# Keeping normalised tokens in SBUF, sending each expert result to its token's home row, and reading the results back with plain transfers

## What is computed

```python
x  = x + attention(...)                      # x2 in the kernel, B*N = 4096 tokens
xf = layernorm(x)                            # l2 in the kernel
shared = gelu(xf @ Wfc_s + bfc_s) @ Wproj_s + bproj_s
probs  = softmax(xf @ Wr)                    # 8 experts
topk_p, topk_i = top_k(probs, 2);  topk_p = topk_p / sum(topk_p)
for e in range(8):
    h = gelu(xf @ Wfc[e] + bfc[e]) @ Wproj[e] + bproj[e]
    routed = routed + h * gate[:, e:e+1]     # gate: topk_p of the two chosen experts, else 0
out = x + shared + routed
```

## Time and profile before

| | us |
|---|---|
| runs, median (lowest to highest of 3) | 2877.65 (2874.66 to 2878.85) |
| the profiled execution | 2873.23 |
| its span in the trace | 2871.6 |
| PE busy | 2529.7 (88% of the span) |
| DVE busy | 1781.9 |
| ACT busy | 1677.4 |
| POOL busy | 1298.8 |

### The profile page before, as it was taken

One profiled execution on the slowest core, in us unless ns is written; L12 is line 12 of the kernel. 1 busy time (PEld: TensorE's weight loads), 2 busy tenths in 40 slices (PEclk: granted clock), 3 DMA queues, 4 the chain that ended last, 5 costly groups with the idle time before them and its releaser, 6 DMA issues. The chain is left out here.

```text
span 2871.6 us, 45293 instructions
## 1 busy us (share of the span) xinstructions
PE 2529.7 (88%) x14668; PEld 2066.3 (72%) x14668; DVE 1781.9 (62%) x2388; ACT 1677.4 (58%) x2269; POOL 1298.8 (45%) x800
## 2 busy tenths in 40 slices
PE   1389999999999999999999999868869999999970
PEld 1366776776777677677677767538859999999970
DVE  6247667777776776776776776644455555555543
ACT  2167777777777777777777777653223344444430
POOL 1355355355454444544644543505535434444446
PEclk8699999999999999999999999989979999999985
DMA  7964654555565465555546545429643389999954
GB/s 260 341 180 127 163 144 145 158 148 156 141 165 151 131 165 137 159 151 137 174 133 151 174 126 150 123 57 198 141 143 101 107 292 320 323 317 326 318 189 147
DMA packets 252547, 514.68 MB, mean 179 GB/s; under 512 B 65223, under 2 KB 135547, under 8 KB 245320
## 3 DMA queue, kind: packets, MB, share of 16 engines
q1 hardware_dynamic: 227368, 449.21, 53.6%
q0 software_dynamic: 14608, 54.02, 5.8%
q10 hardware_dynamic: 10512, 10.75, 1.1%
HBM read 319.10 MB, written 89.92 MB: 142 GB/s over the span
## 5 line engine op out<-in xcount | busy, mean ns | idle before, releaser
L646 DVE TENSOR_TENSOR pr_lo<-pr,pr_hi 128x1024 fp32r<-128x1024 f32 x576 | 812.3, 1415 | 496.2 <-ACT pr_hi L708 492.1
L707 ACT ACTIVATE pr<-ps_s 128x1024 f32<-128x1024 f32 x512 | 525.7, 1027 | 412.4 <-PE ps_s L777 356.3
L708 ACT ACTIVATE pr_hi<-ps_s 128x1024 fp32r<-128x1024 f32 x512 | 521.8, 1019 | 0.0
L791 PE MATMUL ps_o<-pr_hi,vA 128*65 128x512 f32 x1152 | 465.1, 404 | 26.6 <-DVE o_sb L592 19.1
L793 PE MATMUL ps_o<-pr_lo,vA 128*65 128x512 f32 x1152 | 455.1, 395 | 0.0
L792 PE MATMUL ps_o<-pr_hi,vC 128*65 128x512 f32 x1152 | 452.9, 393 | 0.0
L506 POOL TENSOR_TENSOR sq<-raw 128x768 f32<-128x768 f32 x96 | 217.1, 2262 | 503.9 <-ACT raw L694 503.9
L508 POOL TENSOR_TENSOR rs<-ss,minus_half 128x12 f32<-128x12 f32 x96 | 235.1, 2449 | 353.0 <-DVE ss L633 353.0
L1476 ACT ACTIVATE ht<-f_ps_h,b 128x256 f32<-128x256 f32 x448 | 187.8, 471 | 339.7 <-PE f_ps_h L1415 339.7
L749 PE MATMUL ps_m<-w_sb,lnT_sb 128*128 128x384 f32 x1728 | 350.3, 339 | 22.9 <-DMA w_sb<-wHead_dram 22.3
L777 PE MATMUL ps_s<-qq_hi,kk 128*128 128x512 f32 x1152 | 362.4, 396 | 7.7 <-DMA qq_lo<-q_lo 7.4
(11 more groups left out here) (173 smaller groups left out, 3873.4 us busy)
## 6 DMA issues: line engine op xcount, KB each, us to landing
w<-w1S_dram SPq DMA_DIRECT2D x164, 512.0 KB, 5.8
lnT_sb<-lnT_dram SPq DMA_DIRECT2D x32, 2304.0 KB, 8.8
w2raw<-in_L_ffn_Wproj SPq DMA_DIRECT2D x80, 512.0 KB, 6.6
qq_hi<-q_hi SPq DMA_DIRECT2D x128, 256.0 KB, 5.8
qq_lo<-q_lo SPq DMA_DIRECT2D x128, 256.0 KB, 6.0
w_sb<-wHead_dram SPq DMA_DIRECT2D x32, 768.0 KB, 10.1
kk<-k_hi SPq DMA_DIRECT2D x64, 288.0 KB, 5.4
kk<-k_lo SPq DMA_DIRECT2D x64, 288.0 KB, 5.5
```

The lines of the kernel that those rows point to most:

```text
L646: v.tensor_tensor(pr_lo[:, d % RING, :], pr[:, d % 2, :], pr_hi[:, d % RING, :].bitcast(F32), ALU.subtract).then_inc(s_lo, 1)
L707: act.activation(pr[:, d % 2, :], ps_s[:, d % 2, :], ACT.Exp, bias=bias)
L708: act.activation(pr_hi[:, d % RING, :], ps_s[:, d % 2, :], ACT.Exp, bias=bias).then_inc(s_exp, 1)
L791: mm(out, upper, pr_hi[:, r, cols], start=k == 0, stop=False)
```

## The change

**Tokens stay in SBUF.** `l2` becomes an array of all 32 x 128 tokens, 257 numbers wide, that lives from `project_out` to `experts`. POOL's store to `tokens`, its waits, and the array `tokens` go. The transposes of shared tiles read `l2` directly, so that SP loads no `xt` for them.

**A home number per row.** Row `n` of `ys` is no longer a slot: choice `k` of token `t` has its home at row `2t + k`, and the pads go behind row 8192. POOL writes these numbers into column 256 of `l2` (an iota of 32-bit integers; once for `k = 0`, and after all 32 scatters of that choice have landed once more for `k = 1`) and scatters straight from `l2` to `routed`, whose rows are now 257 numbers (1,028 bytes). The clearing of `routed` in `attention` becomes two transfers on ACT's queue, the zeros and a column of 10,496 numbers of 4 bytes each for the pads.

**Results go home tile by tile.** DVE copies the two columns of home numbers out of `xt` (a new instruction, 128x2) before each `y`, and POOL sends each `y` with two indirect transfers of 128 rows to `ys`, between its two `lower_w2`. SP's store of `y` goes. New waits: SP's `xt` load waits for the copy of the home numbers in the buffer's former content, the copy waits until the scatter that used that `home` buffer has landed, POOL waits for `y` and `home`.

**The last part reads plainly.** The two results of a token lie side by side in `ys`, so SP reads 256 tokens with one transfer of 512 KB (line 1557 of the changed kernel), and ACT issues the stores to `out`.

**Loops.** The loops over batches in `project_out` and over shared tiles in `experts` are written out.

```diff
@@ attention
-            act.dma_start(routed.rearrange("(t p) d -> p t d", p=P),
+            act.dma_start(routed[:, 0:D].rearrange("(t p) d -> p t d", p=P),
                           zero[:, :].unsqueeze(1).broadcast_to([P, ROWS // P, D])).then_inc(s_clear, 16)
+            act.dma_start(routed[:, D:WIDE].rearrange("(t p) d -> p t d", p=P),
+                          spare[:, :].bitcast(F32).unsqueeze(2), allow_slow_non_contiguous=True).then_inc(s_clear, 16)
@@ project_out
-                    pool.wait_ge(s_l2, b * G + q + 1)
-                    pool.dma_start(tokens_v[bass.ds(b * G + q, 1)].rearrange("g p t d -> p g t d"),
-                                   l2[:, q:q + 1]).then_inc(s_st[q], 16)
...
-                        ins = v.tensor_scalar(l2[:, q, i:i + 1, :], x2[:, tile, :], mv[:, i, 0:1], rstd[:, i:i + 1],
+                        ins = v.tensor_scalar(l2[:, tile, 0:D], x2[:, tile, :], mv[:, i, 0:1], rstd[:, i:i + 1],
@@ experts, SP
-            load_x(tokens_v, 0, 0)
             load_b1(1, None)
...
-                if left >= 2:
+                if shared and m + 2 >= SHARED:
+                    if s == 0:
+                        sp.wait_ge(s_sc, 16 * 2 * TT)
+                    load_x(routed_v, m + 2 - SHARED, s)
+                elif not shared and left >= 2:
                     sp.wait_ge(s_xt, m + 1)
...
+                    sp.sem_inc(s_go, 1)
+                    sp.wait_ge(s_home, m - (SHARED - 1))
+                    load_x(routed_v, m + (2 - SHARED), s)
...
-                if not shared:
-                    sp.dma_start(ys_v[bass.ds(m - SHARED, 1)].rearrange("t p r d -> p t r d"), y[:, s:s + 1]).then_inc(s_ys[s], 16)
@@ experts, POOL
+            for k in range(2):
+                if k:
+                    pool.wait_ge(s_sc, 16 * TT)
+                pool.iota(l2[:, :, D:WIDE].bitcast(I32), pattern=[[2 * P, TT], [0, 1]], base=k, channel_multiplier=2).then_inc(s_num, 1)
+                pool.wait_ge(s_num, k + 1)
+                for tile in range(TT):
+                    pool.indirect_dma_start(out=routed[:, :], out_offset=bass.IndirectOffsetOnAxis(ap=slots[:, k, tile:tile + 1], axis=0),
+                                            in_=l2[:, tile, :], in_offset=None).then_inc(s_sc, 16)
+
+            def scatter(U, s):
+                pool.wait_ge(s_yv, U * 2 + (s + 1))
+                pool.wait_ge(s_home, U * 2 + (s + 1 - SHARED))
+                pool.sem_inc(s_go, 1)
+                for r in range(2):
+                    pool.indirect_dma_start(out=ys[:, :], out_offset=bass.IndirectOffsetOnAxis(ap=home[:, s, r:r + 1], axis=0),
+                                            in_=y[:, s, r, :], in_offset=None).then_inc(s_ys[s], 16)
...
+                        if not (last and s == 1):
+                            lower_w2(1 - s, h, U * 2 + (s + 3 - SHARED))
+                        if h == 0 and not (first and s == 0):
+                            scatter(U - (1 - s), 1 - s)
@@ experts, DVE
+                if (not shared or m == SHARED - 1) and left >= 1:
+                    if not shared and not (isinstance(U, int) and U == S2 and s == 0):
+                        dve.wait_ge(s_ys[1 - s], (U - (S2 - s)) * 32)
+                    v.tensor_copy(home[:, 1 - s, :], xt[:, 1 - s, :, D].bitcast(I32)).then_inc(s_home, 1)
@@ combine
-                for tile in range(2):
-                    for j in range(2):
-                        pool.indirect_dma_start(out=y[:, i, tile, j, :], out_offset=None, in_=ys[:, :],
...
+                    sp.wait_ge(s_sum, 2 * (k - NB + 1))
+                sp.dma_start(y[:, i], ys_v[k]).then_inc(s_y[i], 16)
```

More of the change, by code:

```diff
@@ L346, in attention @@
         zero = t.sb("zero", [P, D])
+        spare = t.sb("spare", [P, ROWS // P], I32)
         gain2 = t.sb("gain2", [P, DH])
@@ L1383, in pair @@
-            def pair(U, last=False):
-                for s in range(1 if last else 2):
-                    for h in range(2):
-                        lower_w2(1 - s, h, U * 2 + (s + 3 - SHARED))
-            with pool.Fori(S2, LAST) as u:
+            for k in range(2):
[6 more added lines that the diff above has]
+                                            in_=l2[:, tile, :], in_offset=None).then_inc(s_sc, 16)
@@ L1389, in _ @@
+            pair(S2, first=True)
+            with pool.Fori(S2 + 1, LAST) as u:
                 pair(u)
-            pair(LAST, True)
+            pair(LAST, last=True)
+            scatter(LAST, 1)
         @block.tensor
```

144 lines of the change are left out of this document (54 added, 90 removed).

## The result

| | us |
|---|---|
| before, median of 20 runs | 2876.37 (2874.66 to 2879.54) |
| changed, median of 20 runs | 2882.16 (2877.78 to 2885.5) |
| ratio | 1.0019, interval 1.0012 to 1.0026 |
| forecast | 2829, range 2814 to 2856 |
| span of the profiled execution, before and changed | 2871.6 and 2881.7 |

A forecast was written before the change was run, and what follows sets the result against it. It took PE, with nearly full DMA engines, to bound routed tiles and project_out, and POOL's gather issues combine. -43.3 - 4.5 - 1.5 + 1.0 + 0 = -48.3 us gave a median of 2829, range 2814 to 2856.

The forecast's parts named there:

- combine: Last part: without POOL's gathers, 48.5 us from the last y to the end, a gain of 43.3, bounds 22 to 51.5.
- The clearing: Start of attention: the added column of 4-byte pieces costs 31 us of DMA time, 1 us of loss, bounds 0 and 15.
- The rival on this: Start of attention: the two-part clearing stretches the first windows by 15 us or somewhat more, 2845; chance 0.03.
- The landing: Routed tiles: a scatter to ys lands in 5.0 us, so PE does not wait for xt; 0 us.
- The threshold: Routed tiles: scatter landing time, 5.5 to 6.7 us, beyond which PE waits; each us over costs 39 us.
- The 2.8 us that were taken for an idle landing: Scatters: time a scatter needs on idle DMA engines, also used for the last y in the combine sum.
- The first rival: Routed tiles: the scatter's landing comes onto PE's path, 0 to 47 us, in the middle 24, 2853; chance 0.22.
- project_out: project_out: POOL's stores and their waits removed, a gain of 4.5 us out of 0 to 6.4.
- The start of `experts`: Start of experts: 512 KB less ahead of w2raw in SP's queue, a gain of 1.5 us, bounds 0 and 4.
- The DMA engines as the bound: Routed tiles: rival that wide rows costing two packets fill the DMA engines, 24 us, 2853; chance 0.05.
- Straight code at no cost: project_out and experts: written-out loops bring or cost nothing, since PE runs full in straight and looped code.

The follow-up runs named there:

- e5: Changed kernel with the column of home numbers cleared at the end of ACT's second attention window, not right behind the zeros; 2864.8 us, ratio 0.9953.
- e10: Kernel with the mendings, and rows of routed and l2 of 272 numbers (1,088 bytes) instead of 257; 2906.31 us.
- e16: Kernel with the mendings, shared tiles 2 to 13 looped on ACT and DVE, and rows of 272 numbers (1,088 bytes); 2836.16 us, ratio 0.9845.
- e3: Changed kernel with four buffers of home numbers instead of two, DVE's and POOL's loops over routed tiles written out; 2865.39 us, ratio 0.996.
- e4: Changed kernel with SP storing the results as before the change, without POOL's scatters; DVE's copy waits for nothing; 2861.01 us, ratio 0.9944.
- e7: Changed kernel with POOL's two scatters ahead of a tile's first lower_w2 instead of between its two halves; 2864.1 us, ratio 0.9951.
- e8: Changed kernel with POOL's wait for l2 put back in project_out, ahead of its next bias sum; 2883.91 us, ratio 1.0019.
- the mendings: Changed kernel with column cleared after the second window, scatters ahead of lower_w2, POOL waiting for l2 in project_out; 2909.8, 2832.03 and 2839.0 us.

## Why the prediction was wrong, step by step

- **`combine`: the number right, -44.9 for -43.3, but by luck: two errors cancel.** From the end of the last `y` to SP's first load are 9.9 us, not 5.5, since a scatter's issue starts 0.8 us after `y` and the change of part takes 5.4 us from the landing (2.4 us after the last issue at 2836.85), not 1.2. From there to the end are 37.0 us, not 43.0, since the engines moved up to 400 GB/s in slices of the stretch where 331 was taken from the routed tiles.
- **The clearing: the step that failed most, 31.5 us for 1.** The pieces were priced as DMA time beside other work, 31 us, bound 15 at the start. That they are issued by an engine which stands while its queue is full was not thought of, though the text named ACT's queue and the 10,512 pieces already in it. The rival on this had the place (the start of `attention`) but neither mechanism nor size. 24.1 us are the issue (e5). Of the other 7.4, 3.9 are a longer wait for `qq_lo`, which goes when the rows are 1,088 bytes apart (e10, e16), 2.2 are the later start of e5's execution, and 1.3 stay open.
- **The landing: the chain was right, its term mis-sized, 21.1 us for 0.** The threshold was put at 5.5 to 6.7 us and the price at 24 us for a landing of 6.7. Measured: 6.8 us and 21.1 us of loss, 0.56 us a tile, so the threshold was near 6.2; e3, e4 and e7 each give the loss back. What failed is the choice of 5.0 for the landing: the nearest row by queue was POOL's own store with 6.7, and it was passed over for SP's transfers with 5.3 and 5.5. The 2.8 us that were taken for an idle landing were misread, too: that row counts SP's loads of `xt` in with the scatters, and the 64 scatters alone have a median of 2.4 us. The first rival, at 0.22, was the case. The Trainium skill (DMA: Bandwidth & Descriptors, "Queues, rings and completion order") says that a DMA engine turns from queue to queue packet by packet; the prediction concluded that by this rule a scatter would land near its idle time, and the trace does not show that: 6.8 us, and 4.5 at the place that e7 gives it.
- **`project_out`: +1.1 for -4.5.** The relief was real (117.1 us in e8, -2.8 against before), but the removed store had also kept POOL apart from DVE. That the earlier trace rows were waits of one engine for another said nothing of what the two would do when they ran together.
- **The start of `experts`: right**, -1.2 for -1.5, and for the reason given: PE's first product comes 5.7 us earlier, but ACT then stands 6.5 us for `w2raw`.
- **The DMA engines as the bound: rightly set aside**, PE is full at a share of 0.99 in e3.
- **Straight code at no cost: nothing in the changed kernel speaks against it.** Whether the slow stretch of 70 us, seen on one chip in three kernels with the mendings, comes from it stays open.

With three small mendings the idea pays on one chip, 2832 and 2839, ratios 0.9846 (0.9831 to 0.9861) and 0.9861 (0.9846 to 0.9876), near the 2829 that the forecast had asked of the change as it was. On another chip the same kernel took 2910, ratio 1.0116, and was slower than the kernel before.

## What to carry to other kernels

Price a transfer's issue on the engine that gives it, not only the data: a transfer of ten thousand small pieces behind another such one holds that engine for tens of microseconds, and behind an empty queue for half of one. When a buffer's release hangs on a landing, take the landing time from the same queue under the same load and, where rows allow, at the same place in the turn, and if the slack is under a microsecond give the buffer two more places before arguing about it. When a wait is removed, look at which two instructions it had kept apart.

## What the runs showed of the hardware

- An issue on ACT's queue stood until some 11,740 and 10,880 pieces of 4 and 1,024 bytes were left in it (for 45.09 and 25.98 us); with rows of 1,028 bytes until 3,500 to 4,100 were, and once until some 860 were.
- 10,496 pieces of 1,024 bytes written 1,028 bytes apart beside the first windows landed after 70.5 to 80.7 us, 1,088 or 1,024 apart after 57.1 to 58.5; 1,028 apart while ACT stood, after 55.3 (changed kernel).
- Indirect transfers of 128 KB from POOL landed after 6.8 us at a DMA share of 0.94, after 4.5 at another place in the tile (e7), and after 2.4 on nearly idle engines.
- A DVE `tensor_scalar` of 0.41 us took up to 2.49 beside POOL's work on SBUF.
- One program ran at 2910 on one chip and at 2832 and 2839 on another, by a stretch of 70 us in which its engines waited for nothing inside the core.
